# Routing worked out inside the shared expert's tiles instead of in a stage of its own

## The reference

```python
logits = xt @ router_w.T + routing_bias          # layer 0; sigmoid, top 2, normalised to sum 1
scores = softmax(xf @ gate_w.T)                  # layer 1; top 2 of the softmax, not normalised
w = zeros(T, E).at[arange(T)[:, None], top_idx].add(top_p)
h = silu(x @ wg[e].T) * (x @ wu[e].T);  y[e] = h @ wd[e].T      # I = 512 (layer 0), 192 (layer 1)
out = shared_expert(x) + sum_e w[:, e] * y[e]                   # shared: 512 (layer 0), 384 (layer 1)
```

## Time and profile before

| | us |
|---|---|
| median of 3 runs (1954.01 to 1958.13) | 1955.09 |
| the profiled execution | 1957.94 |
| its span, first to last instruction | 1956.2 |
| PE busy | 1642.6 (84%) |
| VectorE busy | 1443.0 (74%) |
| ScalarE busy | 1079.1 (55%) |
| GpSimd busy | 422.1 (22%) |
| DMA, whole span | 83 GB/s to and from HBM |

### The profile page before, as it was taken

How to read it: one execution, slowest core, us unless ns; L and a number is a source line. 1 busy time by engine, 2 the same in 40 slices (tenths; PEclk the granted TensorE clock), 3 DMA queues, 4 the chain that set the end, 5 groups by cost and what they waited for, 6 DMA issues and landing times. The chain is left out here.

```text
span 1956.2 us, 42086 instructions
## 1 busy us (share of the span) xinstructions
PE 1642.6 (84%) x15122; PEld 943.6 (48%) x15122; DVE 1443.0 (74%) x2806; ACT 1079.1 (55%) x2186; POOL 422.1 (22%) x541
## 2 busy tenths in 40 slices
PE   3987569989999993767999999999997857989950
PEld 2775359966666661221222222222223647977730
DVE  5776877744444446869999999999972987756657
ACT  1444435533333333524999999999995534534422
POOL 3000226611222222220000000000000115834432
PEclk9998669999999996876999999999998958999975
DMA  6700025521111114331121121121003203444445
GB/s 249 281 1 6 1 72 166 171 74 61 58 60 58 61 39 146 117 94 50 36 62 47 36 62 46 37 62 37 18 25 122 85 1 97 140 124 128 128 135 167
DMA packets 113092, 164.47 MB, mean 84 GB/s; under 512 B 20279, under 2 KB 89789, under 8 KB 110589
## 3 DMA queue, kind: packets, MB, share of 16 engines
q1 hardware_dynamic: 97372, 117.85, 20.1%
q0 software_dynamic: 15520, 43.93, 6.0%
HBM read 89.07 MB, written 72.37 MB: 83 GB/s over the span
## 5 line engine op out<-in xcount | busy, mean ns | idle before, releaser
L1511 DVE TENSOR_REDUCE sa_row_max<-psum 128x1 f32<-128x1024 f32 x512 | 582.3, 1212 | 12.0 <-PE psum L1393 11.9
L1494 ACT ACTIVATE sa_probs<-psum 128x512 f32<-128x512 f32 x1024 | 549.6, 597 | 37.7 <-PE psum L1444 28.2
L1393 PE MATMUL psum<-v_k_max,v_q_stack 48*128 48x512 f16 x1024 | 301.4, 398 | 24.1 <-DVE sa_row_max L1511 16.2
L1424 PE MATMUL psum<-sa_probs,sa_v_now 128*32 128x256 f32 (+1 forms) x3840 | 321.0, 406 | 0.1
L1444 PE MATMUL psum<-v_q_stack,sa_k_main 49*128 49x512 f16 x1024 | 309.8, 385 | 1.9 <-ACT sa_probs L1494 1.4
L1988 PE MATMUL psum<-m0w_all,m0fx_xt_high 128*128 x568 | 192.9, 381 | 0.7 <-DVE m0fx_xt_low L1920 0.7
L1444 PEld LDWEIGHTS psum<-v_q_stack,sa_k_main 49*128 49x128 f16 x1024 | 64.6, 94 | 222.1 <-ACT sa_probs L1494 208.7
L1424 PEld LDWEIGHTS psum<-sa_probs,sa_v_now 128*32 128x32 f32 x3840 | 75.7, 108 | 189.9 <-issue 100.1
L1934 DVE TENSOR_TENSOR m0fx_ht_low<-psum,m0fx_ht_high 128x512 f16<-128x512 f32 x71 | 49.1, 692 | 134.4 <-ACT m0fx_ht_high L1902 134.4
L1317 POOL TENSOR_SCALAR sa_max_half<-sa_o_sb 128x128 f16<-128x128 f32 x32 | 9.2, 289 | 553.1 <-ACT sa_o_sb L1485 553.1
L1879 POOL DMA_INDIRECT y_rows<-m0fx_y_sb,m0s_all x71 | 68.1, 959 | 273.2 <-DVE m0fx_y_sb L1941 273.2
(11 more groups left out here) (349 smaller groups left out, 3377.6 us busy)
## 6 DMA issues: line engine op xcount, KB each, us to landing
x_rows<-la_blank SPq DMA_DIRECT2D x18, 1032.0 KB, 8.8
v_q_stack<-q_scratch SPq DMA_DIRECT2D x192, 64.0 KB, 2.4
m0s_all<-x_rows SPq DMA_DIRECT2D x71, 129.0 KB, 2.0
m1fx_x_in<-x_rows SPq DMA_DIRECT2D x71, 129.0 KB, 2.2
m0fs_stage<-in_up SPq DMA_DIRECT2D x16, 512.0 KB, 4.2
m0g_got<-y_rows SPq DMA_DIRECT2D x32, 256.0 KB, 3.9
o_scratch<-sa_o_sb POOLq DMA_DIRECT2D x32, 256.0 KB, 2.5
wo_o_in<-o_scratch SPq DMA_DIRECT2D x32, 256.0 KB, 3.6
```

Source lines behind the costliest of these rows:

```text
L1393: nc.tensor.matmul(mx_ps[m % 2][:, half * 512:(half + 1) * 512], q_stack[h][side:side + ROWS, head, qt * P:(qt + 1) * P], k_max[side:side ...
L1424: last = nc.tensor.matmul(o_ps[32 * g:32 * g + 32, cols], v_now[:, kt, kv, :], probs[(GROUPS * step + g) % 16][:, cols], start=(kt == 0), ...
L1494: nc.scalar.activation(probs[at % 16][:, :], st_ps[bank_of(at)][:, :], ACT.Exp, scale=0.25 / (QK_SCALE * QK_SCALE)).then_inc(s["expd"], 1)
L1511: nc.vector.tensor_reduce(row_max[n % 2][:, at % QT, column:column + 1], mx_ps[m % 2][:, :], AX.X, ALU.max).then_inc(s["maxed"], 1)
```

## The change

`route` is gone as a stage. A class `Route` issues the same VectorE instructions in six pieces inside `shared_expert`: piece 0 (`choose`: casts, masks of the chosen experts, weights) ahead of slot 0, pieces 1 to 4 at the end of slots 0 to 3, piece 5 (`experts`, for `r.expert_of`) at the end of slot 12. GpSimd's masks come first in its block, ScalarE's Exp first in its block, the two matmuls behind `up(0)`. `both`, `before` and `all_ones` are f16 where they were f32; `ones` for the scans is a tensor of its own. `norm` and `again` no longer go with the slot. Norm 0 to 2 are in slot 4, and from there 1.5 a slot until the old distance (i + 3) is reached. Each `again` stands one slot later than its norm. GpSimd waits for the slots (end of piece 4) before the first copy. All temporaries, `top` and `index` lie in the weight space of experts 4 to 7, which slot 16 is the first to fill.

```diff
-def shared_expert(core, name, w, x_rows, r, w_next, next_dram, filled):
+def shared_expert(core, name, w, x_rows, r, w_next, next_dram, filled, routing):
+    PIECE_AT = {0: (1,), 1: (2,), 2: (3,), 3: (4,), 12: (5,)}
+    FIRST = 4
+    NORMS = [[] for i in range(n + 2)]
+    done = 0
+    for i in range(FIRST, n):
+        upto = min(i + 4, n, 3 + (i - FIRST) * 3 // 2)
+        NORMS[i], done = list(range(done, upto)), upto
+        route = Route(ph, r, *routing)
             def _(pool):
+                route.gpsimd_masks(pool)
                 if filled is not None:
...
+                pool.wait_ge(route.routed, 1)
                 for i in range(n):
...
                 def cut_high(k, u):
+                    if k == E // 2 and u == 0:
+                        act.wait_ge(route.routed, 2)
...
-                    if real(i + 2):
-                        again(i + 2)
+                    for p in NORMS[i - 1] if i >= 1 else ():
+                        again(p)
                     if real(i):
                         hidden_high(i, j)
-                again(0)
-                again(1)
+                route.scalar_exp(act)
                 slots(act, slot)
...
-                    if real(i + 3):
-                        norm(i + 3)
+                    for p in NORMS[i]:
+                        norm(p)
...
                         hidden_low(i, j)
-                for i in range(3):
-                    norm(i)
+                    for piece in PIECE_AT.get(i, ()):
+                        route.vector_piece(dve, piece)
+                route.vector_piece(dve, 0)
                 slots(dve, slot)
...
                         up(lin_ps[j], i, 0).then_inc(s["lined"], 1)
+                    if i == 0:
+                        route.tensor_ranks(pe)
                     if real(i - 1):
                         down(i - 1, 1 - j)
...
+    def tensor_ranks(self, pe):
+        pe.wait_ge(self.masks, 7)
+        pe.wait_ge(self.both_done, 1)
+        flat = self.both.rearrange("p t e -> p (t e)")
+        nc.tensor.matmul(self.rank_ps[:, 0:T * E], self.before, flat, start=True, stop=True)
+        nc.tensor.matmul(self.total_ps[:, 0:T * E], self.all_ones, flat, start=True, stop=True)\
+            .then_inc(self.counted, 1)
...
+    def vector_piece(self, dve, piece):
+        (self.choose, self.count, self.starting, self.first_slots, self.second_slots, self.experts)[piece](dve)
...
-                top = pl.sb("top", [P, T, 8])
-                index = pl.sb("index", [P, T, 8], mybir.dt.uint32)
-                router_logits(core, name + "rl", shared.router, bias_row, top, index)
-                route(core, name + "r", r, normalise, top, index)
-            shared_expert(core, name + "fs", shared.w, x_rows, r, w, (up_r, down_r), filled)
+            late = w.all[:, E // 2:E, :].rearrange("p e f -> p (e f)").bitcast(F32)
+            top = late[:, 0:T * 8].rearrange("p (t e) -> p t e", e=8)
+            index = late[:, T * 8:2 * T * 8].bitcast(mybir.dt.uint32).rearrange("p (t e) -> p t e", e=8)
+            router_logits(core, name + "rl", shared.router, bias_row, top, index)
+            shared_expert(core, name + "fs", shared.w, x_rows, r, w, (up_r, down_r), filled,
+                          (normalise, top, index, late[:, 2 * T * 8:late.shape[1]]))
```

More of the change, by code:

```diff
@@ L3 @@
 from contextlib import ExitStack, contextmanager
+import math
 F32 = mybir.dt.float32
@@ L2050, in __init__ @@
         self.expert_of = ph.sb("expert_of", [P, SLOT_TILES // WORD], I32)
[L2053 to L2153, removed]
-                for e in range(E):
-                    last = nc.vector.tensor_tensor_scan(running[:, :, e], ones[:, 0:T], total[:, :, e], 0.0,
-                                                        ALU.mult, ALU.add)
-                then(last)
-                then(nc.vector.tensor_scalar(count_i[:, :], running[:, T - 1, :], float(P - 1), None, ALU.add))
-                then(nc.vector.tensor_scalar(count_i[:, :], count_i[:, :], P.bit_length() - 1, None,
-                                             ALU.arith_shift_right))
-                then(nc.vector.tensor_copy(n_tiles[:, :], count_i[:, :]))
-                then(nc.vector.tensor_tensor_scan(ends[:, :], ones[:, 0:E], n_tiles[:, :], 0.0, ALU.mult, ALU.add))
-                then(nc.vector.tensor_tensor(starts[:, :], ends[:, :], n_tiles[:, :], ALU.subtract))
-                then(nc.vector.tensor_tensor(slot[:, :, :], running[:, :, :], total[:, :, :], ALU.subtract))
-                then(nc.vector.tensor_tensor(slot[:, :, :], rank_ps[:, 0:T * E].rearrange("p (t e) -> p t e", e=E),
-                                             slot[:, :, :], ALU.add))
-                then(nc.vector.tensor_scalar(starts[:, :], starts[:, :], float(P), None, ALU.mult))
-                then(nc.vector.tensor_tensor(slot[:, :, :], slot[:, :, :],
-                                             starts[:, :].unsqueeze(1).to_broadcast([P, T, E]), ALU.add))
-                for c in range(2):
-                    then(nc.vector.tensor_tensor(picked[:, :, :], chosen[c][:, :, :], slot[:, :, :], ALU.mult))
-                    then(nc.vector.tensor_reduce(slot_f[:, :, c], picked[:, :, :], AX.X, ALU.add))
-                then(nc.vector.tensor_copy(r.slots[:, :, :], slot_f[:, :, :]))
-                then(nc.vector.tensor_tensor(passed[:, :, :], ends[:, :].unsqueeze(1).to_broadcast([P, SLOT_TILES, E]),
-                                             tile_iota[:, :].unsqueeze(2).to_broadcast([P, SLOT_TILES, E]), ALU.is_le))
-                then(nc.vector.tensor_reduce(expert_f[:, :], passed[:, :, :], AX.X, ALU.add))
-                then(nc.vector.tensor_scalar(expert_f[:, :], expert_f[:, :], float(E - 1), None, ALU.min))
-                pairs = expert_f[:, :].rearrange("p (k c) -> p k c", c=2)
-                then(nc.vector.scalar_tensor_tensor(out=packed[:, :], in0=pairs[:, :, 1], scalar=float(E),
-                                                    in1=pairs[:, :, 0], op0=ALU.mult, op1=ALU.add))
-                pairs = packed[:, :].rearrange("p (k c) -> p k c", c=2)
-                then(nc.vector.scalar_tensor_tensor(out=fours[:, :], in0=pairs[:, :, 1], scalar=float(E ** 2),
-                                                    in1=pairs[:, :, 0], op0=ALU.mult, op1=ALU.add))
-                pairs = fours[:, :].rearrange("p (k c) -> p k c", c=2)
-                then(nc.vector.scalar_tensor_tensor(out=r.expert_of[:, :], in0=pairs[:, :, 1], scalar=float(E ** 4),
-                                                    in1=pairs[:, :, 0], op0=ALU.mult, op1=ALU.add))
@@ L2318, in mixture @@
             w = Weights(pw, E, F)
-            with Phase(nc, name + "l") as pl:
-                top = pl.sb("top", [P, T, 8])
-                index = pl.sb("index", [P, T, 8], mybir.dt.uint32)
-                router_logits(core, name + "rl", shared.router, bias_row, top, index)
-                route(core, name + "r", r, normalise, top, index)
-            shared_expert(core, name + "fs", shared.w, x_rows, r, w, (up_r, down_r), filled)
+            late = w.all[:, E // 2:E, :].rearrange("p e f -> p (e f)").bitcast(F32)
[4 more added lines that the diff above has]
+                          (normalise, top, index, late[:, 2 * T * 8:late.shape[1]]))
             space = shared.w.all[:, 0, :].bitcast(F32) if F > 256 else None
```

126 lines of the change are left out of this document (added).

## The result

The changed kernel takes 1964.01 us in the median of five runs (1963.53 to 1966.69), the kernel before 1955.78 on the same chip (1954.01 to 1958.13). The ratio is 1.0039, with a 95% interval of 1.0028 to 1.0049: 0.4% slower. The profiled execution took 1963.53 us, for 1957.94 before.

What follows compares the result with a forecast made beforehand. TensorE was taken to bound layer 0's shared expert, with VectorE close, and GpSimd was full in layer 1. 1957.94 + 1 (layer 0) + 5 (layer 1) gave 1963.9 profiled, 2.85 less for a median of 1961; range 1952 to 1967.

Steps and rivals of the forecast that it cites:

- rival 4: The forecast itself: GpSimd's late start decides layer 1, layer 0 is a draw; 1957 to 1965 us, chance 0.45.
- Pieces 1 to 4 cost 4.3 of it up to tile 4: Layer 0, VectorE: 6.25 us of pieces behind tiles 0 to 3 lose 4.3 us, leaving 7.8 of the lead.
- Slot 6 waits for c1(0) and c1(1): Layer 0: norms 4 and 5 wait for scatters to land in four buffers; slot takes 7.1 us for 3.3.
- Slots 8, 10 and 12 wait 0.3 to 1.5 us each: Layer 0: these slots hold two norms and wait again for landings, 0.3 to 1.5 us each.
- Clock taken at nothing: TensorE's half speed after holes: 0 to +1.5 us a layer, taken as 0, hidden under VectorE's delays in tiles 0 to 3.
- Slots ready in layer 1 21.1 us after routing's start, second scatter at 25.3: Layer 1: slots ready at 1634.3, tile 0's second scatter on GpSimd at 1638.5, 8.3 us later than before.
- Pace 2.95 us a tile: Layer 1, GpSimd's scatters: 31 tiles at 2.95 us, so next loads +5 us; bounds 2.72 (-2) to 3.05 (+8).
- TensorE idle 8 us or more at the end of layer 1's stage: Layer 1: TensorE, some 8 us ahead, finishes by 1721 and idles until the last row lands; lead worth nothing.
- The median lies 2.85 below the profiled execution: Whole kernel: 2.85 us taken off the profiled forecast of 1963.9 to get a median of 1961.
- Rival 1: Hole comes off and GpSimd catches up, at 2.72 us a tile in layer 1: faster, 1949 to 1950 us, chance 0.15.
- Rival 2: Gain and loss cancel: pace of 2.8 us, layer 0 within 3 of zero; 1952 to 1958 us, chance 0.25.
- Rival 3: Four buffers too few in layer 0 with landings of 5 us or more: +6, layer 1 +5; 1966 us, chance 0.15.

Runs made afterwards that it cites:

- all0_held6_gap5: all0_held6 with piece 5's six instructions issued one by one in slots 6 to 11; 1951.59 us, ratio 0.9968 to the kernel before.
- early_slots: Changed kernel with pieces 0 to 4 and norms 0 to 2 ahead of slot 0, then one norm a slot; 1952.56 us, 0.9979 of the kernel before.
- early_held6: early_slots with six row buffers for four in layer 0; 1953.79 us, ratio 0.9982 to the kernel before.
- held6: Changed kernel with six row buffers for four in layer 0; 1956.79 us, ratio 0.9998 to the kernel before.
- early_warm: early_held6 with 120 matmuls, their result overwritten, added on TensorE behind up(1); 1948.13 us, ratio 0.9950 to the kernel before.
- all0_held6: early_held6 with tile 0 put ahead of pieces 1 to 4, which all stand in slot 0; 1952.26 us, ratio 0.9978 to the kernel before.
- early_warm_gap5: early_warm with piece 5's six instructions issued one by one in slots 6 to 11; 1946.54 us, ratio 0.9942 to the kernel before.

## Why the prediction came out as it did

The forecast was rival 4's: slower, since GpSimd's late start decides layer 1, and layer 0 a draw. The mechanism was right in layer 1. In layer 0 the waits came where I had put them, but it was no draw: it lost 2.4 us, nearly as much as layer 1. The sum of +6 for the profiled execution measured +5.6 (1957.94 to 1963.53), and that it came so close is luck: it is made of +2.4 and +2.7 with a small rest where I had put +1 and +5, two errors that go opposite ways. Step by step, times from routing's start in brackets, c0(p) and c1(p) for the first and second scatter of tile p:

- *Hole off, hidden_low(0) 12.1 us earlier.* The expert's matmuls begin at 262.21 (forecast 261.8), and hidden_low(0) is at 8.87 for 21.42, 12.5 earlier. Right.
- *Pieces 1 to 4 cost 4.3 of it up to tile 4.* hidden_low(4) forecast at 290.8 (29.3), measured 290.58 (28.4): 3.8 lost. Right.
- *Slot 6 waits for c1(0) and c1(1).* norm(4) was to go at 296.6 and went at 296.69; norm(5) at 299.5 and went at 298.88 (c1(1) took 3.0 us to land, not 4.2). hidden_low(8) forecast at 311.0, measured 311.86. Right: of the 8.8 us that layer 0 was ahead at tile 4, 3.4 were left at tile 8.
- *Slots 8, 10 and 12 wait 0.3 to 1.5 us each.* This term was mis-sized. Slots 8 and 10 were near, with 1.45 + 1.43 and 1.34. In slot 12 norm(14) waited 3.48, for a scatter issued at 322.71 and landed at about 329.0: 6.2 us, the longest of the layer, where I had used the median of 4.2 everywhere. One slow landing in front of a queue without slack costs its whole excess. It is not one draw of bad luck either: the three other runs with this order of norms waited 3.2, 4.3 and 3.3 us in the same slot. hidden_low(14) came at 341.52 (79.3) for the forecast 338.5 (77.0).
- *Piece 5 nearly all paid, 2.4.* all0_held6_gap5 priced it at 2.2. Right.
- *Clock taken at nothing.* Not wholly so in layer 0: 291 to 295 was granted 0.57 behind a hole of 2.19 us, and 332 to 336 0.57 behind the hole of slot 12, where piece 5 kept VectorE late as well. How much it cost in the changed kernel stays open. I had looked for it after up(1), where the hole was 1.38 us and not 3, and 272 to 288 was granted 1.00.
- *Slots ready in layer 1 21.1 us after routing's start, second scatter at 25.3.* Measured 20.8 and 24.9. Right.
- *Pace 2.95 us a tile.* This term was mis-sized. From 1641.82 to 1732.94, the end of the last, are 91.1 us, 1.19 + 31 x 2.90. By the group's means: copy 0.29, two scatters of 1.02, gaps of 0.58, so 2.91. 31 x 0.05 = 1.6 us of the 2.4 by which layer 1's +5 was too large is this; 0.4 is the earlier start, 0.7 the way from the last scatter's end to the loads, 1.9 us where I had 2.6, and 0.2 goes the other way, as the first of these scatters took 1.19 for 1.0.
- *TensorE idle 8 us or more at the end of layer 1's stage.* 10.44. Right. But its lead over the kernel before was not the 8 us that I had kept: 8.4 at tile 4, 5.3 at tile 14, 4.6 at the last. Piece 5 lies between (tiles 12 to 14 take 8.4 us for 5.7), and four waits for landings, 4.3 us, that I had not counted in a layer with eight buffers. Behind a late GpSimd this cost nothing.
- *The median lies 2.85 below the profiled execution.* This step failed. It was the chance of one execution, not a property of the kernel: after the change the profiled execution lies 0.5 us below its median, in early_slots 3.6 above (1956.16), in early_held6 1.4 below (1952.42). This is what puts 1961 three us under the measured 1964.01, although the profiled execution came within 0.4 of its forecast.

**The rivals.** Rival 1 (GpSimd at 2.72 in layer 1) fell: behind its second scatter GpSimd waited for no row, and its pace was 2.90. The lock-step with TensorE that spoke for it was there only in part: 2.99 before, beside tiles of the same pace, and 2.90 now that it runs by itself. Rival 2 needed a pace of 2.8. Rival 3, four buffers too few, is what layer 0 bears out in kind: six buffers took 5.0 us off it (held6), and the landing of slot 12 took over 5 us. Its own sum, +6 there, was too high by 3.6. The outcome is thus the forecast's in layer 1 and lies between forecast and rival 3 in layer 0.

By the Trainium skill, page "SBUF — State Buffer", section "Who interferes with whom", a VectorE instruction in a two-port mode that issues first holds the port pair that it shares with GpSimd for the whole instruction and the other waits, and one with two SBUF inputs contends with a GpSimd instruction that reads SBUF. The runs agree in kind: the scatter that takes 0.96 to 0.98 at its shortest took 1.32 and 1.19 in the rows above, while VectorE ran cut_low, and 1.02 in the mean, and the copy 0.29 for 0.19. What that adds up to, 2.90 for 2.72, had to be measured.

By the Trainium skill, page "DMA: Bandwidth & Descriptors", section "Anatomy of one DMA — SWDGE (gpsimd) path", such a DMA takes about 2.0 us and the time of its bytes at 436 GB/s, which for 132 KB gives an estimate of 2.3 us. With the 1 us of GpSimd's instruction that is 3.3. Layer 1 lies between the two in the median (2.4 to 3.9 from issue to landing, median 2.8), layer 0 above both (2.5 to 6.2, median 3.9). Why the layers differ no run here shows; the number of buffers had to be chosen by the slow end, not by such a fit.

## What to carry to other kernels

Before you fill a hole, look for the engine that has no slack behind it: an engine that starts later ends later by as much, less the slack that it had and what a quicker pace gives back, whatever the hole gave the others. Here GpSimd's second scatter went 8.0 us later, its last ended 5.0 us later and the stage 2.7. Work moved into a loop's slots is paid there unless it is cut into the loop's own gaps, and a wait for a landing wants buffers for the slowest landing, not for the median; six for four were not quite enough here. And where TensorE must idle for several us ahead of dense work, try matmuls without a use in that time, as early_warm did.

## What the runs showed of the hardware that I had not expected

After 8 us of idle time TensorE was granted 0.50 for some 6 us although it had nothing but matmuls to do, and 120 matmuls without a use in that idle time brought 3.2 us in layer 0 and 1.6 in layer 1. In all0_held6 the clock was at 0.50 behind 6.07 us of idle time. Shorter holes went either way: in the changed kernel one of 2.83 us was followed by 0.57 (332 to 336) and one of 2.19 us by 0.57 (291 to 295), while 1.45 us before the first down in early_warm and 1.87 us in layer 1 of early_warm_gap5 were followed by 1.00 (277 to 283 and 1625 to 1631). The holes differ in what stood around them as well, so no run here gives the length that matters. How long the lower level lasts varies too: layer 1 is the same in early_slots and early_held6, and the 6 us behind its first down were granted 0.50 in one and 0.71 in the other, whose stretch was 1.2 us shorter.

The lower level can hide other costs: in early_slots it covered a wait of 2.85 us for a landing, so that removing the wait alone showed nothing. Removing the half speed alone, with four buffers kept, was not tried.
